# Second attention of a four-layer stack: scores of each head from its own 32-row group, and where the causal masks are added

## What is computed

```python
q = (x @ wq).reshape(bsz, seqlen, NH, HD).transpose(0, 2, 1, 3)      # NH = 32, HD = 8
k = (x @ wk).reshape(bsz, seqlen, NKV, HD).transpose(0, 2, 1, 3)     # NKV = 8
v = (x @ wv).reshape(bsz, seqlen, NKV, HD).transpose(0, 2, 1, 3)
k = jnp.repeat(k, rep, axis=1); v = jnp.repeat(v, rep, axis=1)       # rep = 4
att = jnp.einsum('bhqd,bhkd->bhqk', q, k) / math.sqrt(HD)
att = jnp.where(mask[None, None, :, :], -jnp.inf, att)               # mask: keys after the query
att = jax.nn.softmax(att, axis=-1)
y = jnp.einsum('bhqk,bhkd->bhqd', att, v)
return y.transpose(0, 2, 1, 3).reshape(bsz, seqlen, NH * HD) @ wo
```

## Time and profile before

| what | value |
|---|---|
| median of three runs | 1650.41 us |
| span of the profiled execution | 1650.5 us |
| PE, DVE, ACT, POOL busy, share of the span | 92%, 61%, 41%, 22% |
| second attention, first scores to last output | 1262.97 to 1460.51 us |

### The profile page before, as it was taken

How to read it: one execution, slowest core, us unless ns; L and a number is a source line. 1 busy time by engine, 2 the same in 40 slices (tenths; PEclk the granted TensorE clock), 3 DMA queues, 4 the chain that set the end, 5 groups by cost and what they waited for, 6 DMA issues and landing times. The chain is left out here.

```text
span 1650.5 us, 20846 instructions
## 1 busy us (share of the span) xinstructions
PE 1523.2 (92%) x7619; PEld 1074.8 (65%) x7619; DVE 1012.1 (61%) x1903; ACT 674.3 (41%) x1300; POOL 363.2 (22%) x258
## 2 busy tenths in 40 slices
PE   7999999999899868997996899899889999989998
PEld 5788888877767534666885355455664555547887
DVE  6777777721422798245445789898455777744444
ACT  1354555410221240202322699896442555533221
POOL 3100000000401323104005079497661000000000
PEclk9999999999899889989998989899988999999999
DMA  5200000040421400014551022131001333001222
GB/s 189 74 14 19 13 16 16 7 127 22 144 92 56 137 0 1 1 51 166 202 168 52 27 75 99 45 103 64 17 1 29 91 98 84 18 1 53 58 58 64
DMA packets 93906, 105.26 MB, mean 64 GB/s; under 512 B 13909, under 2 KB 77513, under 8 KB 93694
## 3 DMA queue, kind: packets, MB, share of 16 engines
q1 hardware_dynamic: 90750, 95.86, 19.3%
q0 software_dynamic: 3072, 8.30, 1.6%
HBM read 83.39 MB, written 14.55 MB: 59 GB/s over the span
## 5 line engine op out<-in xcount | busy, mean ns | idle before, releaser
L997 POOL TENSOR_TENSOR m_state_c<-m_state,m_c 128x1024 f32<-128x1024 f32 x64 | 153.4, 2399 | 84.9 <-DVE m_state L2896 68.8
L2896 DVE TENSOR_TENSOR_SCAN m_state<-m_decay,psum 128x512 f32<-128x512 f32 x128 | 149.0, 1207 | 14.5 <-POOL m_state_c L997 9.6
L3044 DVE TENSOR_REDUCE a_max_pieces<-psum 128x4 f32<-128x512 f32 (+2 forms) x176 | 107.7, 638 | 52.1 <-PE psum L1764 29.9
L2254 ACT ACTIVATE a_probT<-psum 128x512 f32<-128x512 f32 (+1 forms) x176 | 97.4, 559 | 89.5 <-PE psum L1791 86.0
L1632 PE MATMUL psum<-m_state_c,ident 128*128 128x512 f32 x256 | 121.3, 596 | 3.8 <-POOL m_state_c L997 3.8
L1113 PE MATMUL psum<-ones_bf,ident_bf 128*128 128x512 bf16 x287 | 77.3, 429 | 20.6 <-DVE xn L2354 4.9
L940 POOL TENSOR_TENSOR rstd<-var_eps,half_neg 128x4 f32<-128x4 f32 x18 | 20.2, 1121 | 341.9 <-DVE var_eps L2340 341.7
L2185 ACT ACTIVATE m_b_inputT<-m_dtuT,m_bcT 128x256 f32<-128x256 f32 x218 | 93.1, 496 | 0.6 <-PE psum L1624 0.5
L2605 DVE TENSOR_TENSOR f_h<-f_silu,psum 128x512 f32<-128x512 f32 (+1 forms) x46 | 31.5, 686 | 99.8 <-ACT f_silu L2005 99.1
L2005 ACT ACTIVATE f_silu<-psum 128x512 f32<-128x512 f32 (+1 forms) x46 | 27.5, 597 | 158.6 <-PE psum L1296 158.6
L1624 PEld LDWEIGHTS psum<-ident,m_b_inputT 128*128 128x128 f32 x512 | 62.0, 151 | 42.5 <-DVE m_state L2896 35.2
(11 more groups left out here) (457 smaller groups left out, 3544.9 us busy)
## 6 DMA issues: line engine op xcount, KB each, us to landing
f_fc<-in_L_ffn_fc_w_dram SPq DMA_DIRECT2D x16, 1024.0 KB, 6.1
m_c<-m_c_rows SPq DMA_DIRECT2D x32, 512.0 KB, 3.7
f_share<-f_share_rows SPq DMA_DIRECT2D x32, 256.0 KB, 3.3
f_out_rows<-f_out SPq DMA_DIRECT2D x15, 256.0 KB, 2.2
f_slot_rows<-f_out SPq DMA_DIRECT2D x1, 2560.0 KB, 9.8
f_rows_in<-f_slot_rows SPq DMA_DIRECT2D x10, 256.0 KB, 3.1
wkv<-in_L_attn_Wk_dram SPq DMA_DIRECT2D x16, 128.0 KB, 2.2
wkv<-in_L_attn_Wv_dram SPq DMA_DIRECT2D x16, 128.0 KB, 2.2
```

The lines of the kernel that those rows point to most:

```text
L997: pool.tensor_tensor(hc2[c][:], h2[c][:], c_wide[v][:].rearrange("p (b s) -> p b s", b=BATCH), ALU.mult).then_inc(s_hc, 1)
L2254: act.activation(probT3[n % 2][:, PROB3[i]:PROB3[i] + wide], bank[TURNED3[at % 3]][:, 0:wide], ACT.Exp).then_inc(s_exp3, 1)
L2896: ins = dve.tensor_tensor_scan(h2[c][:, b], dec2[c][:, b], bank[4 + 2 * c + b], 0.0, ALU.mult, ALU.add)
L3044: dve.tensor_reduce(max_of3[n % 2][:, int(diagonal), t_, heads[0]:heads[-1] + 1], o, AX.X, ALU.max).then_inc(s_max3, 1)
```

## The change

Each head gets a 32-row group of the stacks of its own. Rows 32j to 32j + 23 hold head j's query parts (high, low, high) and the key's (high, high, low), rows 32j + 24 and 25 the two parts of its maxima against -1, and the rest is -1. A stack of keys is now 512 columns wide instead of 4 x 512. A matmul of `scores` takes the 24 rows of one head, one of `turned_scores` its 26.

Both products use one list of 12 jobs a unit: for each head the query tile 3 (512 columns), then for each head tiles 2 and 0 together (384 + 128), then for each head tile 1 (256). No mask matmul is left on PE. In `maximum` DVE adds a mask that is 0 but for the diagonal block, and takes the maximum, in one `tensor_tensor_reduce` per tile. In the new `mask` DVE adds a turned 128 x 128 mask in place to the diagonal block of each tile in the bank, before ACT takes the exponent. `max_rows` loses its first step.

The maxima's way into the stack changes: ACT copies the turned rows from bank 7 (`copy_rows`), and SP sends them to the strided partitions in two transfers (`place_rows` on SP), which `turned_scores` waits for. The parts of queries and keys go to DRAM first (`keep_parts`, 18 transfers), and a stack comes back in two transfers of 256 KB. Near the start of the program SP fills the unused rows of the DRAM copies with -1, by two transfers of together 1.25 MB from a tile that POOL sets. POOL's clearing of the stacks goes; two masks are made instead. `LEAD3` is 8 instead of 3; the `attend` pieces stand at steps 3, 5, 7 and 9.

```diff
+        PIECES3 = ((3,), (2, 0), (1,))
+        JOBS3 = [(j, PIECES3[c]) for c in range(3) for j in range(REP3)]
...
-        LEAD3, STACKS3 = 3, 4
...
+        LEAD3, STACKS3 = 8, 4
...
+            unused = minus_ones[0:GROUPS3 * REP3].broadcast_to([GROUPS3 * REP3, DH3 * TOK // DM, DM])
+            sp.dma_start(q_rows3[:, :, MAX_ROW3:].rearrange("g j r c -> (g j) r c"), unused).then_inc(s_cleared, 16)
+            sp.dma_start(k_rows3[:, MAX_ROW3:], unused[0:GROUPS3]).then_inc(s_cleared, 16)
...
+                if tile_ is None:
+                    for c, part in enumerate((k_high3, k_high3, k_low3)):
+                        sp.dma_start(k_rows3[:, DH3 * c:DH3 * (c + 1), toks], part[:, toks].bitcast(F32)).then_inc(stored, 16)
+                else:
+                    for c, part in enumerate((q_high3, q_low3, q_high3)):
+                        dst = q_rows3[4 * tile_:4 * tile_ + 4, :, DH3 * c:DH3 * (c + 1), toks].rearrange("g j d c -> (g j) d c")
+                        sp.dma_start(dst, part[:, tile_, toks].bitcast(F32)).then_inc(stored, 16)
...
+                sp.dma_start(q_stack3[u][:].bitcast(F32), q_rows3[g, :, :, toks].rearrange("j r c -> (j r) c")).then_inc(s_stack3[u], 16)
+                sp.dma_start(k_stack3[u][:].bitcast(F32), k_rows3[g, :, toks].unsqueeze(0).broadcast_to([REP3, ROWS3, SEQ])).then_inc(s_stack3[u], 16)
...
+            def place_rows(n):
+
+                sp.wait_ge(s_mcopied3, COPIED3_0 + n + 1)
+                for c in range(2):
+                    first = MAX_ROW3 + c
+                    sp.dma_start(q_stack3[n % STACKS3][first:first + ROWS3 * (REP3 - 1) + 1:ROWS3, :].bitcast(F32),
+                                 max_rows3[n % 2][REP3 * c:REP3 * (c + 1), :].bitcast(F32)).then_inc(s_mrow3, 16)
...
+            for b in range(BATCH):
+                sp.wait_ge(s_low3, 2 * b + 2)
+                keep_parts(None, b, s_parts3[b][0])
+                keep_parts(0, b, s_parts3[b][0])
+            for b in range(BATCH):
+                sp.wait_ge(s_parts3[b][0], s_parts3[b][1] + PARTS3)
+                stack(b)
+            for b in range(BATCH):
+                sp.wait_ge(s_low3, 4 + b + 1)
+                keep_parts(1, b, s_parts3[2][0])
+            for n in range(2, STACKS3):
+                stack(n)
+            sp.wait_ge(s_parts3[2][0], s_parts3[2][1] + PARTS3)
             for n in range(UNITS3):
...
+                place_rows(n)
+                if n >= 1 and n + 3 < UNITS3:
+                    sp.wait_ge(s_scT3, NJ3 * n)
+                    stack(n + 3)
+                for dst, src, loaded in loads3[2 * n:2 * (n + 1)]:
+                    sp.dma_start(dst, src).then_inc(loaded, 16)
...
-                for i in range(STACKS3 + 2):
-                    clear_stack(i)
+                ch.step(pool.memset(mask_wide3[:], 0.0))
+                ch.step(pool.memset(mask_turned3[:], 0.0))
                 ch.step(pool.memset(sumsq[:], 0.0))
...
-                        if n % 2 and STACKS3 + 2 + n // 2 < 3 * STACKS3:
-                            pool.wait_ge(s_ssq, n + 1)
-                            clear_stack(STACKS3 + 2 + n // 2)
...
-                    t_, heads, diagonal = MAX_JOBS3[i]
...
+                    j, pieces = JOBS3[i]
+                    at, u, r, column = NJ3 * n + i, n % STACKS3, slice(ROWS3 * j, ROWS3 * j + MAX_ROW3), 0
...
-                        mm = pe.matmul(o, ident_bf[:], mask_bf[:].unsqueeze(1).broadcast_to([P, len(heads), P]),
-                                       start=False, stop=True)
+                    for t_ in pieces:
+                        wide = (t_ + 1) * P
+                        mm = pe.matmul(bank[SCORES3[at % 3]][:, column:column + wide], q_stack3[u][r, t_ * P:(t_ + 1) * P],
+                                       k_stack3[u][r, 0:wide], start=True, stop=True)
+                        column += wide
                     mm.then_inc(s_sc3, 1)
...
-                    t_, heads = JOBS3[i]
...
+                    j, pieces = JOBS3[i]
+                    at, u, r, column = NJ3 * n + i, n % STACKS3, slice(ROWS3 * j, ROWS3 * j + MAX_ROW3 + 2), 0
...
-                        pe.wait_ge(s_mrow3, n + 1)
+                        pe.wait_ge(s_mrow3, 32 * (n + 1))
...
+                    for t_ in pieces:
+                        wide, s0 = (t_ + 1) * P, (ST - 1 - t_) * P
+                        mm = pe.matmul(bank[TURNED3[at % 3]][:, column:column + wide], k_stack3[u][r, s0:s0 + P],
+                                       q_stack3[u][r, s0:], start=True, stop=True)
+                        column += wide
+                    mm.then_inc(s_scT3, 1)
...
-                        pe.wait_ge(s_exp3, NJ3 * (n + 1))
+                    pe.wait_ge(s_exp3, NJ3 * n + REP3 * (next(c for c in range(3) if t_ in PIECES3[c]) + 1))
...
-                        if ahead and i == NJ3 - 2:
+                        if ahead and i == NJ3 - 5:
                             turn_max(n + 1)
...
-                        if i in (3, 6) and done:
-                            attend(n - 1, i // 3 - 1)
-                    if done:
-                        attend(n - 1, 2)
-                        attend(n - 1, 3)
+                        if i in (3, 5, 7, 9) and done:
+                            attend(n - 1, (i - 3) // 2)
...
-                    act.wait_ge(s_scT3, at + 1)
...
+                    act.wait_ge(s_sel3, MASKED3_0 + at + 1)
...
+                def copy_rows(n):
+
+                    act.wait_ge(s_mturn3, n + 1)
+                    if n >= 2:
+                        act.wait_ge(s_mrow3, 32 * (n - 1))
+                    act.copy(max_rows3[n % 2][:], bank[7][0:2 * REP3, :]).then_inc(s_mcopied3, 1)
+
+                copy_rows(0)
...
+                            if n + 1 < UNITS3 and i == NJ3 - 5:
+                                copy_rows(n + 1)
...
+                    j, pieces = JOBS3[i]
+                    at, column = NJ3 * n + i, 0
...
-                    dve.tensor_reduce(max_of3[n % 2][:, int(diagonal), t_, heads[0]:heads[-1] + 1], o, AX.X, ALU.max).then_inc(s_max3, 1)
+                    for t_ in pieces:
+                        wide = (t_ + 1) * P
+                        ins = dve.tensor_tensor_reduce(masked3[at % 3][:, column:column + wide], bank[SCORES3[at % 3]][:, column:column + wide],
+                                                       mask_wide3[:, SEQ - wide:], 1.0, START, ALU.add, ALU.max,
+                                                       max3[n % 2][:, t_, j:j + 1])
+                        column += wide
+                    ins.then_inc(s_max3, 1)
...
+                def mask(n, i):
+
+                    at, pieces = NJ3 * n + i, JOBS3[i][1]
+                    dve.wait_ge(s_scT3, at + 1)
+                    for c in range(len(pieces)):
+                        block = bank[TURNED3[at % 3]][:, (ST - 1) * P * c:(ST - 1) * P * c + P]
+                        ins = dve.tensor_tensor(block, block, mask_turned3[:], ALU.add)
+                    ins.then_inc(s_sel3, 1)
...
-                    ch.step(dve.tensor_tensor(m[:], pieces[:, 0], pieces[:, 1], ALU.max))
-                    ch.sync()
...
-                def place_rows(n):
...
-                    dve.tensor_copy(q_stack3[n % STACKS3][96:96 + 2 * REP3, :], bank[7][0:2 * REP3, :]).then_inc(s_mrow3, 1)
...
+                def next_maximum(at):
+
+                    if at < NJ3 * UNITS3:
+                        maximum(at // NJ3, at % NJ3)
+                        if at % NJ3 == NJ3 - 1:
+                            max_rows(at // NJ3)
...
+                for at in range(NJ3 + LEAD3):
+                    next_maximum(at)
+                for n in range(UNITS3 + 2):
                     for i in range(NJ3):
+                        next_maximum(NJ3 * (n + 1) + LEAD3 + i)
...
-                            maximum(n, i)
-                        if i == LEAD3 - 2 and 1 <= n <= UNITS3:
-                            place_rows(n - 1)
...
-                    if n < UNITS3:
-                        max_rows(n)
+                            mask(n, i)
+                        if i == 4 and n >= 2:
+                            outputs(n - 2)
```

More of the change, by code:

```diff
@@ L282, in build @@
         x_high0 = Region(here + DM * 4, KT * TOK * 4).take("a0_x_high", [P, KT, TOK], F32R)
[L283 removed]
+        minus_ones = Region(here + DM * 4 + KT * TOK * 4, DM * 4).take("a3_minus_ones", [P, 1, DM])
+        assert here + 2 * DM * 4 + KT * TOK * 4 <= w_odd.end
         slotted(ffn0, w, CAP0, ffn0.routed)
@@ L582, in build @@
         max3 = [we.take(f"a3_max{u}", [P, ST, REP3]) for u in range(2)]
-        max_of3 = [we.take(f"a3_max_pieces{u}", [P, 2, ST, REP3]) for u in range(2)]
+        masked3 = [we.take(f"a3_masked{u}", [P, SEQ], BF16) for u in range(3)]
+        mask_wide3 = we.take("a3_mask_wide", [P, SEQ])
+        mask_turned3 = we.take("a3_mask_turned", [P, P])
+        max_rows3 = [we.take(f"a3_max_rows{u}", [2 * REP3, SEQ], F32R) for u in range(2)]
```

(3 more changed lines are left out.)

140 lines of the change are left out of this document (42 added, 98 removed).

## The result

The changed kernel takes 1721.93 us (median of four runs, 1720.22 to 1722.5) beside 1650.37 us for the kernel before: a ratio of 1.0429, 95% interval 1.0414 to 1.0444. It is slower by 71.6 us where 12.5 were forecast, and outside the range. The profiled span grows from 1650.5 to 1719.7 us, by 69.2; the launch with the second span took 1721.61 us, so about 1.9 us lie outside a span, which the forecast, comparing a span with a median, had put at nothing.

The account below looks back on a forecast made before the run. The prediction took PE to bound the kernel before and DVE after: 12.5 us a unit against 11.70 gave the stage +12.2 us; with +1.5 for the fill and -1.2 for POOL's clearing, +12.5 on 1650.5, so 1663 us, range 1640 to 1700.

Parts of the forecast that it names:

- the first price: PE's score products in the attention: 20 products of 512 columns, 0.23 us apart, 4.6 us a unit.
- PE stops being the bound: Attention: without mask products PE needs 8.3 us a unit, if weight loads stay hidden, against 11.70 for a unit before.
- the nine tenths: Sign against the forecast: PE still busy above nine tenths; it expected PE idle for a fifth or more.
- PE as the bound, but through weight loads: Attention: changing row groups exposes 32 weight loads of 0.196 us, 14.6 us a unit, 1693 us; chance 0.08.
- DVE's sum: DVE's work in an attention unit: sums with maximum, reads, masks, `max_rows` and `outputs`, together 11.86 us.
- the first rival: DVE's reads nearly free (0.035 us each), nobody waits for the maxima: 11.2 us a unit, 1644 us; chance 0.22.
- The wait for the maxima: PE waiting for the maxima's rows before `turned_scores`: 0.6 us a unit, between 0 and 1.5.
- The fill: Filling DRAM rows with -1 near the start delays the first attention's weights: +1.5 us, between 0 and 3.8.
- POOL's clearing: Removing POOL's clearing beside the feed-forward block shortens the time: -1.2 us, between 0 and -1.6.
- The new pairs don't overlap: DVE's new attention instructions run without overlap: 1689 us if only reads wait, about 1710 if all do; chance 0.15.

Follow-up runs that it names:

- planes: Changed kernel with each head's keys in a zero-filled plane, 128 rows a product, earlier maxima, fill behind the first weights: 1657.32 us beside 1650.91 for the kernel before.
- one row group: Changed kernel with all score products of a unit on rows 0 to 23 (or 25) of the stacks: 1761.89 us.

## Why the prediction was wrong

*The step that failed* is the first price: "Consecutive products of 512 columns start 0.23 us apart: 20 x 0.23 = 4.6 us", and with it "PE stops being the bound". Those rows are of 128-row products at 1.00. The products that the change puts in their place use 24 or 26 rows, and under them the clock goes to 0.50 and stays. By PE's timeline from start to start, in the twelve equal units, the score products take 8.8 us where the forecast had 4.6, the values 4.9 instead of 2.4, the turns 2.0 instead of 1.3: 15.7 us a unit on PE instead of 8.3, and PE 95% busy, which is above the nine tenths that the forecast had named as a sign against it. The forecast asked whether PE would be busy and for how long, and took the clock as given; its list of rivals had PE as the bound, but through weight loads, at 1693. That rival's premise was not quite so either: with `LEAD3` = 8 and four heads, the two products of one step belong to the same head and row group, and the group changes only from step to step; no run tried another order. That the height of the products is the cause is shown by four runs: 128 rows with the instructions, order and waits unchanged bring 0.89, planes 0.97, while one row group and 64 rows leave 0.50. What in the height it is stays open: 24, 26 and 64 rows lie on one side, 96 and 128 on the other, and no run tells the number of rows from the use of a part of the array as such. The Trainium skill, "TensorE: Matmul & The Clock Gate", section "Part 1: The HAM clock gate", has the clock follow how busy PE has been; here PE was 95% busy at 0.50, so that by itself would have forecast 1.00, and the measurement decides.

*DVE's sum*, 11.86 us, was too high by 1.0: the reads cost nothing (the first rival's price), the sums with maximum 6.6 instead of 6.38. That rival was right about the reads, and it did not matter while PE was slow. At full clock, in the version with planes, the unit is 11.53, 0.7 above the rows' 10.85.

*The wait for the maxima*, 0.6 us: 1.6 us at the higher clock with 128 rows, and there it costs more than itself, because the clock falls behind it. In the changed kernel it is some 0.6 us a unit of waiting loads (7.4 us in 12 units), beside a PE that is late anyway.

*The fill*, +1.5 with 3.8 as its upper bound: 8.4 by the lag, 7.2 by the run that moves it. Bytes over the best rate were no upper bound: the weights that start PE stand behind the fill, and slack was read from a row in which the weights still came in time.

*POOL's clearing*, -1.2 with -1.6 as its bound: -2.9, by the lag over that block (7.7 to 4.8). The bound took PE's one named wait; but seven of the sums on DVE got shorter, by up to 1.3 us each, and the chain through them with it. That POOL's work is what stretched them is read from the times at which they fall; no run puts the clearing back alone.

*The new pairs don't overlap*, the second rival: refuted. In the rows of DVE above each instruction starts before the one ahead of it has ended, by some 0.07 to 0.1 us. The rule that the forecast cites, in the Trainium skill, "VectorE: DVE Perf Modes", section "Two Vector instructions with no wait between them", holds none of them back, and the trace agrees.

## What to carry to other kernels

Before a product is cut to fewer rows of the array, ask what clock it will be granted: busy time at 0.50 looks like busy time at 1.00, and only the clock's column and the distance between the starts of like products tell them apart. Keep products in a long stretch at full height, with zero rows if need be, and do not put low and full ones in turn. When masks move from a bound engine to another, moving half of them can be worth more than moving all: here 1642.48 beside 1655.51 for the kernel before, against 1657.32 beside 1650.91.
